# A graph kernel on one Trainium2 core: in passes one and two GpSimd waits, at every fifth pair of gathers, for the landing of the pair it issued last

## What is computed

```python
# layer 0: attention with 8 heads of 32
q = feat @ Wq.T + bq;  k = feat @ Wk.T + bk;  v = feat @ Wv.T + bv
score = clip(sum_d(q[dst] * k[src]) / sqrt(32), -10, 10)
ex    = exp(score - segment_max(score, dst)[dst])
alpha = ex / segment_sum(ex, dst)[dst]
y     = segment_sum(alpha * v[src], dst) @ Wp.T + bp
x0    = feat + y
h     = gelu(layernorm(x0) @ W1.T + b1) @ W2.T + b2
x     = layernorm(x + (x0 + h))
# layer 1: additive attention, normalised over the source
z     = leaky_relu((x @ W_s.T)[src] + (x @ W_t.T)[dst], 0.2)
e     = z @ W_attn.T
alpha = softmax of e over the edges of one src
agg   = segment_sum(x[src] * alpha, dst)
x     = layernorm(x + (agg @ W_fc.T + b_fc))
```

## Time and profile before

| what | value |
|---|---|
| median of 3 runs without the profiler | 3276.47 us (3273.84 to 3283.2) |
| span of the profiled execution | 3995.8 us |
| time of the profiled execution outside its span | not listed; the page gives the span alone |
| GpSimd busy | 1960.5 us, 49% of the span |
| VectorE busy | 2175.4 us, 54% |
| TensorE matmul busy | 2303.1 us, 58% |
| ScalarE busy | 1124.8 us, 28% |
| mean granted TensorE clock | 0.761 |
| bytes moved by DMA | 698.62 MB |

### The profile page before, as it was taken

The page is one execution under the profiler, slowest core; times in us unless marked ns, Lnnn a source line. Parts: engine busy times, 40 slices in busy tenths (PEclk is TensorE's granted clock), DMA queues, the critical chain, the costliest instruction groups (busy, mean ns, idle before and its releaser), DMA issues.

```text
span 3995.8 us, 54572 instructions
## 1 busy us (share of the span) xinstructions
PE 2303.1 (58%) x11454; PEld 1677.2 (42%) x11455; DVE 2175.4 (54%) x6197; ACT 1124.8 (28%) x2699; POOL 1960.5 (49%) x1970
## 2 busy tenths in 40 slices
PE   4456666666666664878233333333334395777776
PEld 2244444444444443756122222222122294656655
DVE  5455655556555564242344444444444596677676
ACT  0144554445544553333111111111112100111111
POOL 0255555555555553121566666666656303544443
PEclk9788877788778877988666666667666656988898
DMA  4666656666666663121677777777767505666564
GB/s 141 195 179 178 182 176 180 175 180 181 177 178 176 176 177 100 50 86 47 191 215 221 212 211 214 211 214 228 210 206 216 175 0 186 205 197 204 183 208 150
DMA packets 365707, 698.62 MB, mean 175 GB/s; under 512 B 77317, under 2 KB 247039, under 8 KB 365674
## 3 DMA queue, kind: packets, MB, share of 16 engines
q0 software_dynamic: 134784, 425.63, 36.1%
q1 hardware_dynamic: 220602, 256.40, 20.6%
q10 hardware_dynamic: 10288, 16.23, 1.1%
HBM read 597.23 MB, written 100.85 MB: 175 GB/s over the span
## 4 chain that ended last, share of the span: by engine, by line
another core or an unknown queue 27%; PE 26%; DVE 24%; issue 16%; DMA 3%; DVEq 2%; SPq 1%; POOL 1%; ACT 1%; ACTq 0%; POOLq 0%
PE ps_px L900 7%; DVE sb_prod L1622 4%; DVE sb_wide L1615 4%; DVE sb_score L1468 4%; PE ps_pa L913 3%; PE ps_px L913 2%; PE ps_px L998 2%; PE ps_px L1007 2%; PE ps_pa L1058 2%; PE ps_pn L1045 2%; DVE sb_wide L1477 1%; PE ps_px L876 1%; DVE sb_parts L1814 1%; DVE sb_prod L1462 1%
## 5 line engine op out<-in xcount | busy, mean ns | idle before, releaser
L900 PE MATMUL ps_px<-sb_parts 128*128 x2430 | 468.2, 358 | 798.8 <-DVE sb_wide L1615 563.1
L900 PEld LDWEIGHTS ps_px<-sb_parts 128*128 128x128 bf16 x2430 | 268.1, 122 | 999.4 <-DVE sb_wide L1615 625.6
L779 POOL DMA_INDIRECT sb_ring<-kv_rows,sb_idx x324 | 322.5, 995 | 357.8 <-DVE sb_wide L1477 152.6
L913 PE MATMUL ps_pa<-sb_wide,sb_onehot 128*128 128x264 f32 x864 | 302.8, 483 | 317.1 <-DVE sb_wide L1477 256.2
L779 POOL DMA_INDIRECT sb_ring<-proj_rows,sb_idx x324 | 316.5, 977 | 303.8 <-issue 170.8
L779 POOL DMA_INDIRECT sb_parts<-kv_rows,sb_idx x324 | 316.0, 975 | 206.9 <-DVE sb_wide L1477 107.4
L1142 ACT ACTIVATE sb_parts<-sb_bits,sb_nn_tab 128x768 bf16<-128x768 int16 x135 | 126.3, 937 | 1016.6 <-remote 606.9
L900 PE MATMUL ps_px<-sb_parts,sb_xwm 128*128 x2430 | 397.9, 309 | 19.2 <-ACT sb_xwm L1147 14.6
L779 POOL DMA_INDIRECT sb_w<-narrow_rows,sb_idx x324 | 315.3, 973 | 163.7 <-issue 102.2
L913 PE MATMUL ps_px<-sb_wide,sb_onehot 128*128 128x264 f32 x756 | 252.9, 466 | 197.3 <-DVE sb_wide L1477 124.3
L779 POOL DMA_INDIRECT sb_w<-feat_rows,sb_idx x162 | 158.9, 981 | 416.0 <-issue 192.3
(11 more groups left out here) (256 smaller groups left out, 4473.2 us busy)
## 6 DMA issues: line engine op xcount, KB each, us to landing
sb_bits<-dst_short SPq DMA_DIRECT2D x280, 192.0 KB
x_edges<-sb_ring SPq DMA_DIRECT2D x54, 768.0 KB
sb_slots<-x_edges SPq DMA_DIRECT2D x54, 768.0 KB
x_edges<-sb_slots SPq DMA_DIRECT2D x27, 768.0 KB
sb_w<-x_edges SPq DMA_DIRECT2D x27, 768.0 KB
sb_msg<-lo_rows SPq DMA_DIRECT2D x28, 576.0 KB
kv_rows<-sb_slots ACTq DMA_DIRECT2D x25, 256.0 KB, 2.8
sb_parts<-part_rows SPq DMA_DIRECT2D x28, 193.5 KB
```

Of the source, the lines that this page charges most:

```text
L779: pool.indirect_dma_start(out=out[:, i, :], out_offset=None, in_=rows, in_offset=bass.IndirectOffsetOnAxis(ap=idx[:, 2 * p + i:2 * p + i + ...
L900: mm = pe.matmul(into, hots_t[L][:, 2 * p + i, :], flat(visit_parts[:, bass.ds(parity, 1), a, 0:width]), start=(a == 0), stop=(a == 2))
L913: mm = pe.matmul(into[:, 0:C + H], onehot[:, j, :], sums_in[:, 2 * (p % FLIGHT) + i, :], start=(p % EARLY == 0 and i == 0), stop=True, ski ...
```

## The change

After the pairs p = 4, 9 and 14 of each visit (SLOTS = 5, so `p % SLOTS == SLOTS - 1`) GpSimd waits until both gathers of that pair have landed, and then adds one to `pool_seen`, a counter that nobody waits for. This is done in pass one and in pass two.

```diff
@@ gathers_kv
                         slot_free(0, v, p)
                         gather_pair(0, p, kv_pairs[p], kv_rows, gathered[p])
+                        if p % SLOTS == SLOTS - 1:
+                            landed(pool, 0, total, v, p)
+                            pool.sem_inc(pool_seen, 1)
@@ gathers_proj
                         slot_free(1, v, p)
                         gather_pair(1, p, proj_slots(p), proj_rows if streamed(p) else narrow_rows, gathered[p])
+                        if p % SLOTS == SLOTS - 1:
+                            landed(pool, 1, total, v, p)
+                            pool.sem_inc(pool_seen, 1)
```

## The result

The changed kernel takes **3845.7 us**, the kernel before 3277.1 us beside it: a ratio of 1.173 with a 95% interval of 1.172 to 1.175, or 569 us slower. The direction was as forecast; the size lies above the range, which ended at 3760 us.

The account below looks back on a forecast made before the run. The prediction took GpSimd's gather issue in both passes as the bound. 160 waits x 2.6 = 416 us less 45 us of slack gave +371 on 3276, rounded to 3650 us; range 3330 to 3760 us.

Parts of the forecast that it names:

- What bounds the kernel: Passes one and two: GpSimd's gather issue, one each 1.25 us, at least 1012 us per pass, bounds the timed runs.
- the missing 719 us: Whole kernel: profiled span 3995.8 us against timed 3276; the difference was taken as idle stretches absent from timed runs.
- The slack of 45 us (0 to 90): Passes one and two together: time left above GpSimd's 2025 us of issue, subtracted from the cost of the waits.
- The length of a wait, 2.6 us with an upper bound of 2.8: Pass one, each added wait: landing 2.1 plus restart 0.81 less usual gap 0.30 us; lower bound 1.7.
- 3.1 us a wait and 3727 us in all: Both passes: alternative price with the skill's 2.6 us landing counted from the instruction's end, +451 us; not used.
- in the shadow of the wait: Each added wait: its register instruction and semaphore increment hide behind the landing; otherwise 48 us at most.
- Pass two at the same 2.6 us: Pass two, each wait: engines empty 1.9 us after the last gather, SyncE's transfers included; 2.6 us taken as well.
- The sum: Both passes: 160 waits x 2.6 = 416 us, less 45 us, +371 us on 3276, rounded to 3650 us.
- A: Passes one and two: waits absorbed in time GpSimd already waits, giving 3276 to 3400 us; chance 0.15.
- B: Passes one and two: forced emptying of transfers shortens VectorE's standstills, -80 us, 3196 us; chance 0.08.
- C: Pass one: added idling keeps TensorE's clock low and TensorE becomes the bound, about 3920 us; chance 0.05.
- The signs named in advance: Profile after: gaps of 2.6 to 3.2 us or more in nearly all 160 places; profiled passes change less than timed.

Follow-up runs that it names:

- d5: Kernel before plus, in pass two only, a GpSimd addition of 768 numbers per partition where the change waits, no landing wait: 3452.6 us, before 3274.5.
- f1: Changed kernel with each wait aimed at the landing of the pair issued two pairs earlier: 3278.5 us, kernel before 3274.3.
- d4: Changed kernel with the waits moved to p = 2, 7 and 12: 3916.2 us, kernel before 3269.8.
- c2: Kernel before, unedited, run again for a profile (c2_before_again): 4023 us beside 4020, ratio 1.000.
- c1: The changed kernel run again, unedited, on a chip where the kernel before takes 4020.0 us: 4067.8 us, ratio 1.013.
- c3: Kernel before plus a GpSimd addition of 768 numbers per partition at the change's places in both passes, no landing wait: 3974.5 us, before 4020.0.

## Why the prediction was wrong

**What bounds the kernel** was right, against the profile it was read from. What got it right was the accounting of the missing 719 us: less pass three's share, it left GpSimd's issue as the bound. d5 and f1 show it: passes of 1064 and 1037 us in which GpSimd hardly waits.

**The slack of 45 us (0 to 90)** was mis-sized: it is nil. The two passes have 1064 + 1037 = 2101 us on a quick chip, 76 above my 2025, and this is nearly all longer gathers. I took the 0.95 us of single rows; the mean is 810.10 / 810 = 1.00 us in pass one and 782.46 / 803 = 0.97 in pass two. With the gap of 0.30 this makes 1053 + 1029 = 2082 us and not 2025. The of before had it: 798.49 / 810 = 0.99.

**The length of a wait, 2.6 us with an upper bound of 2.8**, is the step that failed. It is 3.6 us: 3.5 in pass one and 3.8 in pass two. Of its two parts the landing was the larger error. I had 2.1 us; by the semaphore it is 2.7 us in pass one. The 2.1 rested on two readings. One was the moment at which the DMA engines run empty, and the semaphore comes 0.34 us after the last packet. The other was VectorE's start at 802.13, which says nothing of this landing: the gather at 799.21 fills `sb_parts`, and VectorE's instruction reads `sb_ring`, a pair gathered long before. Even the trace of the kernel before has semaphore updates of transfers up to 802.96, 2.8 us after 800.16, though it does not say whose. The other price that the prediction worked out and set aside, 3.1 us a wait and 3727 us in all, was nearer. The restart was 0.81 us and is 0.97, or 1.37 at the end of a visit, 1.1 on the mean. The 0.81 holds for the wait that it came from, GpSimd's for a place. Here one more wait with its instructions stands ahead of the next gather, and at p = 14 the loop's branch does. I had counted these instructions as lying "in the shadow of the wait"; the runs fit 0.16 us for them behind it, though none separates them.

**Pass two at the same 2.6 us** failed for one more reason. It came out at 304.5 / 80 = 3.8 us. A wait at p = 4 falls among SyncE's transfers; the timeline of the changed kernel has one with a gap of 5.33 us, then one of 2.75 at p = 9 and 4.01 at p = 14. The first, with SyncE's issues while that pair is under way and VectorE's start on the same landing:

```profile
2406.16 0.41 SPq L546 DMA_DIRECT2D x_edges<-sb_ring  x1
2407.09 0.35 SPq L533 DMA_DIRECT2D sb_parts<-part_rows  x1
2407.10 1.06 POOL L779 DMA_INDIRECT sb_w<-narrow_rows,sb_idx  x1 [0.30 <-issue]
2407.90 0.80 SPq L529 DMA_DIRECT2D sb_bits<-dst_short  x1
2412.61 0.69 DVE L1621 TENSOR_TENSOR sb_wide<-ps_px,sb_w 128x516 f32<-128x516 f32 x1 [3.69 <-DMA sb_w<-narrow_rows,sb_idx]
2413.49 1.04 POOL L779 DMA_INDIRECT sb_w<-narrow_rows,sb_idx  x1 [5.33 <-DVE sb_wide L1621]
...
2428.80 1.04 POOL L779 DMA_INDIRECT sb_w<-narrow_rows,sb_idx  x1 [2.75 <-DVE sb_wide L1621]
...
2445.45 1.00 POOL L779 DMA_INDIRECT sb_ring<-proj_rows,sb_idx  x1 [4.01 <-DVE sb_wide L1621]
```

The releaser named is VectorE, since its wait for the same landing ended beside GpSimd's. VectorE starts 0.1 us after the landing and GpSimd 0.97. I had put SyncE's part at "some tenths". The pairs at p = 4 and p = 9 have rows of the same 258 floats, and land after 4.56 and 1.84 us: 2.7 us more where SyncE's transfers run beside them. No run moves these transfers away, so that they are the cause is read from this and from d4, and not tried. Rows of half the length do save some tenths, as I had said, and rather more: 1.84 us against 2.7.

**The sum** with the measured gaps: 80 x 3.50 + 80 x 3.84 = 587 us, less 6 us of gathers that are a little shorter than in f1 and the 5 us of gaps that f1 has of its own: 576, for the 577 of the two profiles and the 569 of the timed runs. It had been 416 - 45 = 371. Of what was missing, longer landings are 124 us, longer restarts 48 and the slack 45. The range ended at 3760 because the upper bound of a wait was taken from the same rows as the middle.

**The rivals.** A (absorbed) is not what happened on quick chips, but it is a fair account of pass one on held ones (+5.5 us between c2 and c1). I had tied it to a shorter gap between gathers; that gap is 0.30 us on both kinds. B (faster) is wrong for this edit, yet on held chips shorter stops of GpSimd do clear standstills (-1.0%), with an addition in place of a landing. C is out: in pass one the clock fell from 0.97 to 0.83 (on quick chips; the 0.80 before was a held chip's), in pass two from 0.59 to 0.53, and TensorE's busy time rose by 110 and 37 us under idle time of its own. With the addition in d5 pass two ran at 0.53 too and cost what GpSimd lost, 183 us.

**The signs named in advance.** Gaps in all 160 places came. The forecast was "2.6 to 3.2 us or more"; only those at p = 9 of pass two lie in that stretch, and the others are longer (means of 3.65 to 5.53 us). "The profiled passes change far less than the timed ones" holds between c1 and c2 on one held chip. I could not see that the profile after would come from a quick one.

The Trainium skill, "NOTIFIC — the notification-queue block", section "Overflow: three behaviours, one of which stalls the engine", says that the internal pipeline of the block always holds its producers back rather than lose a record inside the block. The prediction weighed this as the reason of the standstills. In its favour: on held chips they come together with missing records (waits end in "remote" where a quick chip's name a transfer; 2367 matmul records in pass two of c2_before_again for 2430), and in pass two of c3 the standstills and the missing matmul records are gone together. Against it: by that rule the records should all be there; pass two of c3 still lacks most of the transfers' semaphore updates (4591, where d5 has 18068) and runs like a quick one; and quick chips, profiled in the same way, show neither. The runs do not settle it.

## What to carry to other kernels

If an engine issues back to back and is the bound, any wait for something not yet done costs its whole length plus a restart of the engine, here 1.0 to 1.4 us, and nothing hid it here; the same wait aimed two items back was free. Before adding up, check that the profile and the timed runs show the same stage lengths, with a stage that the change does not touch as the gauge. Price a landing up to its semaphore and not up to the moment at which the DMA engines run empty, and be sure that the wait whose end you read is for that transfer. Price the restart from a place with the same instructions behind it, and look at what the other queues transfer at that moment.

## What I had not expected of the hardware

The two conditions: the same program at 3274 us on one chip and 4020 on another, steady within 1% on each, with the sign and size of small edits depending on it (a short stop of GpSimd: +5.4% for one pass on a quick chip, -1.0% for two on a held one). That the held condition's loss in pass two goes away when GpSimd stops for 2.2 us three times a visit, down to the 1220 us of a quick chip. And that GpSimd's restart after a stop is 0.97 us, or 1.37 with the loop's end, whether a landing or its own addition released it, while the same instructions cost nothing when it does not stop.
